# Query projections of seven head groups with seven block products in place of eight, and norm weights loaded by a broadcast

## The reference, cut to what matters

```python
# x, ctx: (8, 128, 512)
h = x + mamba2(rmsnorm(x, ln1_w), ...)
h = h + (silu(h2 @ gate_w.T) * (h2 @ up_w.T)) @ down_w.T      # h2 = rmsnorm(h, ln2_w)
x = layernorm(x + h)
q = (x @ Wq.T) -> 32 heads of 128          # Wq: (4096, 512)
k = (ctx @ Wk.T) -> 8 heads;  v = (ctx @ Wv.T) -> 8 heads
q = rmsnorm(q, q_norm_w); k = rmsnorm(k, k_norm_w)
o = softmax(q @ k.T / sqrt(128) + mask) @ v   # per tile, 4 query heads on each kv head
x = layernorm(x + o @ Wo.T)
x = layernorm(x + lora_moe(x))             # router over 4 experts, the top 2, rank 16
```

## Time and profile before

| | |
|---|---|
| median of 3 runs | 1002.1 us (1001.87 to 1004.43) |
| the profiled execution | 1001.63 us |
| its span | 999.8 us |
| mean granted TensorE clock | 0.991 |
| TensorE matmuls busy | 97% of the span |
| VectorE, ScalarE, GpSimd busy | 57%, 50%, 41% |

### The profile page before, as it was taken

How to read it: one execution, slowest core, us unless ns; L and a number is a source line. 1 busy time by engine, 2 the same in 40 slices (tenths; PEclk the granted TensorE clock), 3 DMA queues, 4 the chain that set the end, 5 groups by cost and what they waited for, 6 DMA issues and landing times.

```text
span 999.8 us, 15461 instructions
## 1 busy us (share of the span) xinstructions
PE 969.1 (97%) x5070; PEld 808.1 (81%) x5070; DVE 572.8 (57%) x1322; ACT 499.8 (50%) x1373; POOL 405.6 (41%) x341
## 2 busy tenths in 40 slices
PE   7998999999999999999999999999999999999896
PEld 5766688788888887888888888888888888888782
DVE  4745553513221366666766666566666666666777
ACT  5756442412132246554654654655555655555554
POOL 4336533844342453342442532622623523514322
PEclk9999999999999999999999999999999999999997
DMA  6200122310111111010020020020020110100002
...
DMA packets 12834, 45.08 MB, mean 45 GB/s; under 512 B 1729, under 2 KB 2369, under 8 KB 9730
## 3 DMA queue, kind: packets, MB, share of 16 engines
...
...
## 4 chain that ended last, share of the span: by engine, by line
PE 89%; DVE 4%; POOL 3%; issue 2%; ACT 2%; DMA 0%; POOLq 0%; SPq 0%; DVEq 0%; ACTq 0%
PE bank L379 25%; PE bank L381 25%; PE bank L380 25%; PE bank L684 5%; PE bank L694 3%; PE bank L390 1%; POOL res L1480 1%; PE bank L490 1%; PE bank L671 1%; DVE bst L1815 1%; POOL h_lo L1362 1%; PE bank L467 1%; PE bank L442 1%; PE bank L455 1%; DVE cbuf L1681 1%
## 5 line engine op out<-in xcount | busy, mean ns | idle before, releaser
L379 PE MATMUL bank<-act_hi,w_hi 128*128 128x512 f32 x560 | 224.4, 401 | 0.3 <-ACT q_t L1167 0.3
L381 PE MATMUL bank<-act_hi,w_lo 128*128 128x512 f32 x560 | 218.6, 390 | 0.0
L380 PE MATMUL bank<-act_lo,w_hi 128*128 128x512 f32 x560 | 218.4, 390 | 0.0
L1551 POOL TENSOR_TENSOR pb<-pb,prec 128x512 f32<-128x512 f32 x64 | 66.6, 1040 | 309.6 <-DVE prec L1950 309.6
L1196 ACT ACTIVATE pb<-pb,nmax 128x128 f32<-128x128 f32 x256 | 99.8, 391 | 78.8 <-DVE nmax L1945 78.8
L379 PEld LDWEIGHTS bank<-act_hi,w_hi 128*128 128x128 f32 x560 | 105.2, 188 | 23.3 <-issue 2.5
L380 PEld LDWEIGHTS bank<-act_lo,w_hi 128*128 128x128 f32 x560 | 105.3, 188 | 23.0 <-issue 2.2
L381 PEld LDWEIGHTS bank<-act_hi,w_lo 128*128 128x128 f32 x560 | 105.1, 188 | 22.5
L379 PE MATMUL bank<-w_hi,ot_hi 128*128 128x512 f32 x256 | 105.0, 410 | 0.8 <-DVE ot_lo L1627 0.8
L381 PE MATMUL bank<-w_hi,ot_lo 128*128 128x512 f32 x256 | 100.9, 394 | 0.0
L380 PE MATMUL bank<-w_lo,ot_hi 128*128 128x512 f32 x256 | 100.3, 392 | 0.0
...
## 6 DMA issues: line engine op xcount, KB each, us to landing
...
res<-in_x SPq DMA_DIRECT2D x8, 256.0 KB, 5.1
raw_b<-in_ctx_t SPq DMA_DIRECT2D x8, 256.0 KB, 3.0
...
```

The costliest lines, as they stand in the source:

```text
L379: mm(o, l_hi, r_hi, start=first, stop=False)
L380: mm(o, l_hi, r_lo, start=False, stop=False)
L381: return mm(o, l_lo, r_hi, start=False, stop=last)
L1551: TT(pb[:, jj % 2, :, :], pb[:, jj % 2, :, :], prec[:, jj % 2, :].unsqueeze(2).to_broadcast([P, GH, L]), ALU.mult).then_inc(p_norm, 1)
```

## The change

**Query projections.** For the groups g = 1 to 7 the projection of a group (512 query features by 1024 tokens over 512 inputs) is cut in two in each direction and computed by seven block products instead of eight (Strassen's algorithm in Winograd's form). A product (`q_prod(gn, i)`, i = 0 to 6) is two outputs m by two k steps by three matmuls, 12 matmuls of 512 columns. The products of group g + 1 stand in the slots 1 to 7 of group g, one each, behind the scores; slot 0 has none. Group 0 keeps its eight plain projections, and the last three of them stand together in slot (0,0). The last group's slots have no query work.

- GpSimd makes the weight sums (`combine_s`, `combine_s1`, `combine_s4`: 4 instructions a group, in the buffer raw_a), splits 7 weight blocks a group and no longer 4, and makes 4 sums of results (`combine_u4`).
- VectorE adds the results: 12 instructions a group (`q_add`) of one bank and one buffer each. ScalarE copies two results to a buffer (`q_copy`), makes the 7 hi halves, and squares out of `q_t` (`q_square`); the copies to `q_t` go.
- The token sums t1 to t4 are made once, in and ahead of group 0: t3 by GpSimd (6 instructions), t1 by VectorE (6), t2 and t4 by GpSimd (4 each), each then with two hi halves on ScalarE (`t_round`) and two lo halves on VectorE (`t_rest`). Product 1 of group 1 waits for t3, product 2 for t2, product 3 for t1, product 6 for t4.
- Scores now stand ahead of the query work in a slot. The weight loads come in blocks of 256 KB as blocks come free; the loads of the expert weights move behind the last product.

**Start.** ln1_w comes by one broadcast load of 256 KB to all partitions, ln2_w and 12 small values by one of 262 KB; `spread_row`, `row_evac` and `keep_clock` are gone.

The core of the diff (indentation cut; TT is a tensor-tensor instruction):

```diff
 load_x(0)
-sp_eng.dma_start(row_one, rows[0:2 * DM].unsqueeze(0)).then_inc(ld_row, 16)
 sp_eng.dma_start(cst[:, 0:P], consts[:, 0:P]).then_inc(ld_small[0], 16)
+sp_eng.dma_start(row_sb[:, 0:DM], rows[0:DM].partition_broadcast(P)).then_inc(ld_small[1], 16)
 load_x(1)
-sp_eng.dma_start(row_sb[:, 2 * DM:], rows[2 * DM:].partition_broadcast(P)).then_inc(ld_small[5], 16)
-sp_eng.dma_start(cst[:, P:], consts[:, P:]).then_inc(ld_small[6], 16)
+sp_eng.dma_start(row_sb[:, DM:], rows[DM:].partition_broadcast(P)).then_inc(ld_small[5], 16)
...
-def spread_row(r):
-def keep_clock(n):
-    for _ in range(n):
-        mm(bank[7][:, 0:P], ident, ident, start=True, stop=True)
...
-pe.wait_ge(ones_set, 1)
-pe.wait_ge(ld_row, 16)
-spread_row(0)
-spread_row(1)
 pe.wait_ge(ld_small[0], 16)
 for i in range(4):
     norm_t(i, (bank[2], bank[3]))
-    keep_clock(10 if i == 3 else 6)
...
-def row_evac(r):
-    act.wait_ge(row_mm, r + 1)
-    A(row_sb[:, r * DM:(r + 1) * DM], bank[4 + r][:, :], ACT.Copy).then_inc(row_ev, 1)
-square(0)
-row_evac(0)
-row_evac(1)
-for i in range(1, 4):
+for i in range(4):
     square(i)
 norm_hi(0, nb)
...
+def prod_rhs(i, k):
+    if i == 0:
+        return act_part(act_hi, k, 1), act_part(act_lo, k, 1)
+    if i in (1, 2):
+        return (t2, t3)[i - 1][k]
+    if i == 3:
+        return t1[k]
+    if i == 4:
+        return act_part(act_hi, 2 + k, 0), act_part(act_lo, 2 + k, 0)
+    if i == 5:
+        return act_part(act_hi, 2 + k, 1), act_part(act_lo, 2 + k, 1)
+    return t4[k]
+def q_prod(gn, i):
+    pe.wait_ge(wq_l, split_at(gn, i) + 1)
+    if isinstance(gn, int) and gn == 1 and i in (1, 2, 3, 6):
+        pe.wait_ge(t_lo, {1: 2, 2: 4, 3: 6, 6: 8}[i])
+    if i == 0:
+        pe.wait_ge(q_ev, 8 * gn)
+        pe.wait_ge(kraw_done, 8 * gn - 2)
+    for m in range(2):
+        if 1 <= i <= 3:
+            pe.wait_ge(qc_done, 6 * gn - 6 + 2 * (i - 1) + m + 1)
+        elif i > 3:
+            pe.wait_ge(q_ev, 8 * gn + 2 * (i - 4) + m + 1)
+        for k in range(2):
+            c0 = WP_COL[i % 2] + (2 * m + k) * P
+            b_hi, b_lo = prod_rhs(swapped(gn, i), k)
+            t = mm3(bank[m][:, :], w_hi[:, c0:c0 + P], w_lo[:, c0:c0 + P], b_hi, b_lo,
+                    k == 0, k == 1)
+        t.then_inc(q_mm, 1)
...
-def slot(g, jj, lead=True, before=True):
+def slot(g, jj, make=True, before=True):
     n, j = jj // HALF, jj % HALF
     pg, pn = (g, 1) if n == 0 else (g + 1, 0)
+    turn = (g, jj + 1) if j < 3 else (pg, 4 * pn)
+    if j == 3:
+        if not is_last(g):
+            kt_step(pg, pn)
+    else:
+        kv_step(pg, pn, j + 1 if j else 0)
+        s_step(*turn)
+    if make and jj:
+        q_prod(g + 1, jj - 1)
+    if not before:
+        q_step(1, 1)
     if j == 0:
-        kv_step(pg, pn, 0)
-    if j < 3:
-        q_step(pg, pn, j + 1)
-        kv_step(pg, pn, j + 1)
-    else:
-        kt_step(pg, pn)
-        if lead:
-            q_step(g + 1, n, 0)
-    s_step(*((g, jj + 1) if j < 3 else (pg, 4 * pn)))
+        kv_step(pg, pn, 1)
+    if not before:
+        q_step(1, 2)
+    if j == 3:
+        s_step(*turn)
     pt_step(g, jj)
+    if not before:
+        q_step(1, 3)
     if before:
         d_step(*((g, jj - 1) if jj else (g - 1, 7)))
     if j == 2:
...
+def wp_hi(gn, i):
+    act.wait_ge(*((ld_q, 16 * gn + 16) if i == 0 else (ld_a12, 16 * gn) if i == 5 else
+                  (ld_a2, 32 * gn) if i == 6 else (s_cmb, 8 * gn - 8 + S_READY[swapped(gn, i)])))
+    act.wait_ge(q_mm, prod_at(gn, i - 2) + 2 if i >= 2 else
+                6 if isinstance(gn, int) and gn == 1 else prod_at(gn, 0) - 2 * i)
+    c0 = WP_COL[i % 2]
+    A(w_hi[:, c0:c0 + 512], quad(BLOCK_AT[swapped(gn, i)]), ACT.Copy).then_inc(wq_h, 1)
 def wo_hi(g, h):
...
+def q_copy(gn):
+    for m in range(2):
+        act.wait_ge(q_mm, prod_at(gn, 0) + m + 1)
+        A(p1_s[m], bank[m][:, :], ACT.Copy).then_inc(qc_done, 1)
...
+def t_round(t, raw, step, seen):
+    for k in range(2):
+        act.wait_ge(step, seen - 1 + k)
+        A(t[k][0], raw[k], ACT.Copy).then_inc(t_hi, 1)
...
+def combine_s(gn):
+    pool.wait_ge(ld_a2, 32 * gn)
+    pool.wait_ge(*((wq_l, 4) if isinstance(gn, int) and gn == 1 else (wo_l, 4 * gn - 2)))
+    TT(quad(A12), quad(A11), quad(A21), ALU.subtract).then_inc(s_cmb, 1)
+    pool.wait_ge(s_cmb, 8 * gn - 7)
+    pool.wait_ge(wq_l, split_at(gn, 0) + 1)
+    TT(quad(A11), quad(A22), quad(A12), ALU.subtract).then_inc(s_cmb, 1)
...
+def combine_u4(gn):
+    pool.wait_ge(qc_done, 6 * gn)
+    for m in range(2):
+        TT(q_t[:, 0, m, :], q_t[:, 0, m, :], u3_s[m], ALU.subtract).then_inc(s_cmb, 1)
+    pool.wait_ge(s_cmb, 8 * gn - 2)
+    for m in range(2):
+        pool.wait_ge(q_ev, 8 * gn + m + 1)
+        TT(q_t[:, 0, m, :], q_t[:, 0, m, :], q_t[:, 0, 2 + m, :], ALU.add).then_inc(s_cmb, 1)
...
+def combine_t2():
+    for k in range(2):
+        pool.wait_ge(t1_step, 5 + k)
+        TT(t2_raw[k], b21[k][0], t1_raw[k], ALU.subtract).then_inc(t_step, 1)
+    for k in range(2):
+        pool.wait_ge(t_step, 7 + k)
+        TT(t2_raw[k], t2_raw[k], b21[k][1], ALU.add).then_inc(t_step, 1)
...
-def slot(g, jj, refill=True):
+def slot(g, jj, make=True):
     n, j = jj // HALF, jj % HALF
     pg, pn = (g, 1) if n == 0 else (g + 1, 0)
     if j == 2:
         k_rsqrt(pg, pn)
+    if make and jj == 1 and not first_group(g):
+        combine_s(g + 1)
+    if make and jj == 4:
+        combine_s4(g + 1)
+    if make and jj < 7 and jj != 1:
+        wp_rest(g + 1, jj)
+    if make and jj == 4:
+        combine_u4(g + 1)
+    if first_group(g) and jj == 1:
+        wp_rest(1, 1)
+        combine_t2()
     p_scale(*((g, jj + 1) if j < 3 else (pg, 4 * pn)))
     if j == 2:
         q_rsqrt(pg, pn)
-    if refill and jj in WQ_SLOT:
-        for h in WQ_SLOT[jj]:
-            wq_rest(g + 1, h)
-    if jj == 0 and not (isinstance(g, int) and g == 0):
-        for h in range(GH):
+    if first_group(g) and jj == 0:
+        combine_s(1)
+    if make and jj == 1:
+        if first_group(g):
+            combine_t4_head()
+        else:
...
+def q_add(gn, i):
+    if i == 5 or i == 1 and swapped(gn, i) == i:
+        dve.wait_ge(s_mm, 8 * gn - 4 if i == 1 else 8 * gn)
+    if i == 4:
+        dve.wait_ge(s_cmb, 8 * gn)
+    for m in range(2):
+        dve.wait_ge(q_mm, prod_at(gn, i) + m + 1)
+        if i < 4:
+            dve.wait_ge(qc_done, 6 * gn - 6 + 2 * (i - 1) + m + 1)
+        if swapped(gn, i) == 3 - i:
+            if i == 2:
+                dve.wait_ge(s_mm, 4)
+                TT(q_t[:, 0, m, :], p1_s[m], bank[m][:, :], ALU.add)
+            TT(u3_s[m], p1_s[m] if i == 1 else u3_s[m], bank[m][:, :], ALU.add).then_inc(qc_done, 1)
+            continue
+        o, first = ((q_t[:, 0, m, :], p1_s[m]), (u3_s[m], q_t[:, 0, m, :]),
+                    (q_t[:, 0, 2 + m, :], u3_s[m]), (q_t[:, 0, m, :], q_t[:, 0, m, :]),
+                    (q_t[:, 1, m, :], p1_s[m]), (q_t[:, 1, 2 + m, :], u3_s[m]))[i - 1]
...
+def combine_t1_dif():
+    dve.wait_ge(n_lo, 24)
+    dve.wait_ge(q_mm, 4)
+    dve.wait_ge(t_step, 4)
+    for k in range(2):
+        TT(t1_raw[k], b11[k][1], b12[k][1], ALU.subtract).then_inc(t1_step, 1)
+    for k in range(2):
+        TT(t1_dif[k], b11[k][0], b12[k][0], ALU.subtract).then_inc(t1_step, 1)
...
+def t_rest(t, raw, base, step, seen):
+    dve.wait_ge(step, seen)
+    for k in range(2):
+        dve.wait_ge(t_hi, base + k + 1)
+        lo(t[k][1], raw[k], t[k][0], t_lo)
```

More of the change, by code:

```diff
@@ L824, in _ @@
             for jj in range(1, 4):
-                slot(last, jj, lead=False)
+                slot(last, jj, make=False)
             pe.wait_ge(kt_ev, 2 * GROUPS)
@@ L2012, in _, with group @@
             softmax_max(0, 0)
-            slot(0, 0, before=False)
-            with dve.Fori(0, GROUPS - 1) as g:
+            t_rest(t3, t3_raw, 0, t_step, 6)
+            def group(g):
                 for jj in range(1, 8):
@@ L2017, in _ @@
                 slot(g + 1, 0)
+            slot(0, 0, before=False)
+            group(0)
+            with dve.Fori(1, GROUPS - 1) as g:
+                group(g)
             def ln2(i):
```

524 lines of the change are left out of this document (364 added, 160 removed).

## The result

| | before | after |
|---|---|---|
| median | 1005.0 us (8 runs, 1001.9 to 1006.5) | 1010.0 us (8 runs, 1008.1 to 1011.4) |
| ratio | | 1.0056, 95% interval 1.0039 to 1.0074 |
| profiled execution, span | 1001.6, 999.8 us | 1011.4, 1009.3 us |

The account below looks back on a forecast made before the run. It took the kernel to be bound by TensorE's matmuls (busy 97% of the span). Terms −19.1 − 3.1 + 12.0 + 0.6 + 1.2 = −8.4 took the median from 1002.1 to 993.7 us, range 984 to 1003.

Parts of the forecast that it names:

- The first term: Query projections: 84 fewer matmuls of 512 columns at 0.2275 us each, −19.1 us if no other engine is late.
- c): First group of attention: TensorE waits for late token sums and softmax work, plus clock spells; +12.0 us (+4 to +20).
- I add 1.3 such spells of 1.5: First group: idle TensorE is followed by 1.3 low-clock spells of 1.5 us, raising 15.2 us of waits to 17.2.
- b): Start of the kernel: first product 4.9 us earlier, less 1.8 for products at half rate; net −3.1 us.
- I take xn at 6: Start: xn, which needs the 256 KB broadcast, begins at 6 us, so the first product comes at about 14.0.
- The end named in the forecast, a start that gains nothing: Start, upper end of its range: 0 us gained if the broadcast is late or weight piece 0 the next wait.
- d): Attention loop: trips fall to 70.07 us with other engines' added work hidden; +0.6 us for all trips, at worst +6.
- the prediction fails if the trip does not fall by 2.7: Attention loop: the forecast's failure sign, against a trip of 72.80 us before and 70.1 expected after.
- the third rival: Loop slots: VectorE becomes the bound through pt_lo in slots with an add pair; time 1010 us, chance 0.10.
- e): Tail, last group: the softmax chain limits it, so 4.3 of 5.5 us lost are kept; +1.2 us (0 to +4).
- The second rival: First group: VectorE's and GpSimd's SBUF reads exclude each other, c) grows by 5, time 999 us; chance 0.25.

Follow-up runs that it names:

- the first two experiments: The changed kernel with the old start, ratio 1.0049; the changed kernel with its broadcast kept and the small matmuls between the first transposes put back, ratio 1.0045.

## Why the prediction was wrong

**The sign was missed by terms that all erred the same way.** The first term (84 matmuls, −19.1) is the count of matmuls times their distance in the rows, and nothing here speaks against it. Against the profiled executions, the others were forecast at +10.7 and came to +28.6. Of that, 4.5 us are the choice of the two executions, since the medians differ by 5.0 and not 9.5. The first row of the table is of this kind, and the profiled execution of before has a granted clock of 0.991 where its runs near the median have 0.988, which is 3 us of 1004.

- **c) The first group: +12.0 forecast, +19.4 measured; the largest miss.** The waits were right: 15.2 forecast, 15.0 in the trace, and place by place 0.95, 2.8, 2.65, 2.9, 3.9, 1.5, 0.5 against 0.75, 2.68, 2.46, 1.84 and 0.16, 3.22, 2.69, 1.13. (The fourth, forecast at the values of tile 2, fell mostly on the query norm sums just ahead of them.) The step that failed is "I add 1.3 such spells of 1.5". There were four, 8.6 us instead of 2, which is 6.6 of the 7.4 that the term missed. The longest lasted from 439 to 449, with a second wait (3.2 us, at product 2) inside a spell that had already begun; the profiles of the first two experiments have such a wait inside a spell too, and it lasts 10 to 11 us there. The run with the waits filled shows the step: without spells the group takes 5.6 us less. I had taken the ratio of waits to spells from one execution of before (two waits, one spell), where chance decides, and applied it to more and longer waits.
- **b) The start: −3.1 forecast, +1.1 in the trace, nothing in the times.** The half pace was right (2.3 us lost, 1.8 forecast). "I take xn at 6" was not: on VectorE xn of tile 0 stands behind the variance of tile 1, and that tile of x landed at 7.2 to 8.4 us in the nine profiles with the broadcast ahead of it, against 5.5 to 7 with the old start. So xn came at 8.1 to 9.4, the first product at 16.4 to 17.7 where no small matmuls were added and not at 14.0, and the half pace took back the 1.2 to 2.5 us that this won. I gave the load a price on the engines that wait for it, and none on the loads behind it in SP's queue. The end named in the forecast, a start that gains nothing, is what came.
- **d) The loop: +0.6 forecast, +4.9 measured**, a trip of 70.7 to 71.3 instead of 70.17. TensorE waits 0.17 us for pt_lo in slot 0 and more of its runs begin anew (some 18 starts of 0.31 us or more in a trip instead of 12). These starts are not priced anywhere in the forecast. By its own sign ("the prediction fails if the trip does not fall by 2.7") this term failed: trips fell by 1.5 to 2.1. VectorE did not become the bound: its 54.7 us are what I forecast, and the third rival's mechanism did not come. That its number, 1010, is the measured one is luck. GpSimd's 42.7 us are 2.0 over the forecast 40.7; I had taken its sums at 1.04 us like p_scale, and they took 1.3 each.
- **e) The tail: +1.2 forecast, +3.2 measured.** In the changed kernel TensorE waits 1.7 us for the key norm, now asked for one slot earlier, and 2.5 for pt_lo, where the kernel before waits 0.9 for scores and 1.6 for p_scale. The stretch that the forecast named, from the scores of slot (7,1) to the transposes of slot (7,4), took 22.8 us and not some 4 less than 23.3. The term is the same in all kernels with the change (group 7 and the tail take 92.2 to 92.8 us), so it is no chance; no run tried this part, and its cause is open beyond these waits.

The second rival (reads that exclude each other) was right as a mechanism: rests of 1.4 to 1.8 us next to 0.68. It was inside my numbers for the waits, and these came as forecast, so it does not explain the miss.

The range failed for the same reason as the forecast. It stopped at 1003, although the ends in its own text, +20 in c), +6 in d), +4 in e) and 0 at the start, reach 1013. Each end was taken as rare by itself. I think that they share a cause, a schedule packed more tightly that is late in more places; that is an argument, not shown.
